# Hyperbolic attention scores on one NeuronCore: the heads' curvature multiplied on GpSimd between two logarithms, in a pipeline with one more stage

## What is computed

```python
def _hyp_attn(q, k, v, curv):
    eps = 1e-06
    tq = jnp.sqrt(1.0 / curv + jnp.sum(q * q, axis=-1, keepdims=True))
    tk = jnp.sqrt(1.0 / curv + jnp.sum(k * k, axis=-1, keepdims=True))
    inner = jnp.einsum('bhtd,bhsd->bhts', q, k) - tq * jnp.swapaxes(tk, -1, -2)
    arg = jnp.maximum(-curv * inner, 1.0 + 1e-07)
    dis = jnp.sqrt(1.0 / curv) * jnp.arccosh(arg)
    scores = 1.0 / (eps + dis) + _causal_bias(...)
    return jnp.einsum('bhts,bhsd->bhtd', jax.nn.softmax(scores, axis=-1), v)
```

## Time and profile before

| | |
|---|---|
| median of 3 runs | 2722.36 us (2722.34 to 2725.09) |
| the profiled execution, its own time | 2718.13 us |
| its span | 2715.2 us |
| busy share PE, DVE, ACT, POOL | 80%, 55%, 52%, 25% |
| granted TensorE clock, mean | 0.839 of full speed |

### The profile page before, as it was taken

The page is one execution under the profiler, slowest core; times in us unless marked ns, Lnnn a source line. Parts: engine busy times, 40 slices in busy tenths (PEclk is TensorE's granted clock), DMA queues, the critical chain, the costliest instruction groups (busy, mean ns, idle before and its releaser), DMA issues. The chain is left out here.

```text
span 2715.2 us, 30081 instructions
## 1 busy us (share of the span) xinstructions
PE 2184.6 (80%) x10649; PEld 840.3 (31%) x10649; DVE 1506.0 (55%) x3298; ACT 1399.8 (52%) x2019; POOL 687.9 (25%) x717
## 2 busy tenths in 40 slices
PE   3799867668999885777898988767799998676689
PEld 1223332124433242222443234212344233321244
DVE  2564456666555255675655625557565543566642
ACT  1245437894234534798324454579632455378932
POOL 1012212332411212233331121133233122123324
PEclk9699876678999986667899988567799998766889
DMA  4200230102500023000431002310051001301012
GB/s 132 65 19 2 69 85 18 34 1 60 137 21 19 1 79 94 25 9 1 114 95 27 1 17 77 79 34 0 5 146 59 19 2 55 93 25 34 1 44 89
DMA packets 67846, 128.32 MB, mean 47 GB/s; under 512 B 11396, under 2 KB 24836, under 8 KB 63076
## 3 DMA queue, kind: packets, MB, share of 16 engines
q1 hardware_dynamic: 67696, 126.40, 16.9%
HBM read 109.99 MB, written 15.20 MB: 46 GB/s over the span
## 5 line engine op out<-in xcount | busy, mean ns | idle before, releaser
L1322 DVE TENSOR_REDUCE mx<-ps 128x1 f32<-128x512 f32 (+3 forms) x1248 | 639.6, 552 | 445.1 <-PE ps L664 346.6
L1070 ACT ACTIVATE pr<-ps 128x1024 f32<-128x1024 f32 (+3 forms) x672 | 515.7, 804 | 435.6 <-PE ps L734 433.4
L661 PE MATMUL ps<-kop,qop 72*128 72x512 bf16 (+6 forms) x1248 | 441.6, 376 | 141.2 <-DVE mx L1322 110.9
L734 PE MATMUL ps<-qop,kop 75*128 75x512 bf16 (+7 forms) x1344 | 408.3, 369 | 113.9 <-DVE wb L1382 40.9
L1609 POOL TENSOR_SCALAR_AFFINE_SELECT pr<-pr 128x512 f32<-128x512 f32 x224 | 146.6, 655 | 833.8 <-ACT pr L1070 833.4
L780 PE MATMUL ps<-pr,vt 128*32 128x512 f32 (+3 forms) x2688 | 344.4, 590 | 6.9 <-POOL pr L1609 6.1
L1129 ACT ACTIVATE pr<-ps 128x512 f32<-128x512 f32 x224 | 133.8, 597 | 343.8 <-PE ps L887 280.2
L661 PEld LDWEIGHTS ps<-kop,qop 72*128 72x128 bf16 (+1 forms) x1248 | 124.2, 102 | 525.1 <-DVE mx L1322 334.2
L734 PEld LDWEIGHTS ps<-qop,kop 75*128 75x128 bf16 (+1 forms) x1344 | 122.2, 105 | 353.0 <-ACT pr L1070 132.1
L897 PE MATMUL ps<-pr,w_down 128*128 128x512 f32 x384 | 197.8, 600 | 3.1 <-POOL pr L1600 3.1
L664 PE MATMUL ps<-maskqk,identb 128*128 128x128 bf16 x832 | 199.0, 247 | 0.0
(11 more groups left out here) (309 smaller groups left out, 2976.3 us busy)
## 6 DMA issues: line engine op xcount, KB each, us to landing
wb<-gates_scratch SPq DMA_DIRECT2D x192, 256.0 KB, 3.4
kop<-kparts_scratch SPq DMA_DIRECT2D x32, 576.0 KB
qop<-qparts_scratch SPq DMA_DIRECT2D x96, 192.0 KB
on<-hmax_scratch SPq DMA_DIRECT2D x8, 1024.0 KB, 5.7
kparts_scratch<-on SPq DMA_DIRECT2D x12, 256.0 KB, 2.9
qparts_scratch<-on SPq DMA_DIRECT2D x12, 256.0 KB, 4.4
qparts_scratch<-wb SPq DMA_DIRECT2D x12, 192.0 KB
kparts_scratch<-wb SPq DMA_DIRECT2D x12, 192.0 KB
```

The costliest lines, as they stand in the source:

```text
L661: mm = pe.matmul(o, qop[0:k, slot(l, u), j, qb * P:(qb + 1) * P], kop[0:k, slot(l, u), j, k0:k0 + wd], start=True, stop=not diag)
L734: mm = pe.matmul(o, kop[0:k, slot(l, u), 2 * pair + j, kb * P:(kb + 1) * P], qop[0:k, slot(l, u), 2 * pair + j, q0:q0 + wd], start=True, s ...
L1070: nc.scalar.activation(pr[:, g % 3, 2 * pair:2 * pair + 2, o0:o0 + wd], ps[:, bank:bank + 2, o0:o0 + wd], ACT.Exp).then_inc(a.exps, 1)
L1322: ins_ = nc.vector.tensor_reduce(mx[:, nth(l, u) % 2, j, qb, col % 2:col % 2 + 1], ps[:, bank, 0:wd], AX.X, ALU.max, negate=True)
```

## The change

`hyp_score` is split. In `hyp_log` ACT takes the first logarithm over both heads; POOL multiplies each head by its factor and adds eps (two `tensor_scalar` of up to 128x512, one semaphore step each, `h_lin`); in the new `hyp_score` ACT takes the second logarithm over both heads without scale or bias, then the exponential. `hyp_log` stays at p+2, the rest goes one position later: `hyp_score` and `hyp_shift` to p+3, `hyp_exp`, `hyp_cut` and `hyp_values` to p+4. On POOL the new pair stands behind the cuts and ahead of the add. The ring keeps five buffers. The outputs of the hyperbolic unit move from positions 12 and 28 to 13 and 29. The number of positions stays at 37, since three ordinary units set it. In the setup, ahead of all batches, two semaphores are folded into others.

```diff
-POSITIONS = (UNITS * NS, max(3 * NS, HYP_POS[-1] + 4) + 1)
+POSITIONS = (UNITS * NS, max(3 * NS, HYP_POS[-1] + 5) + 1)
...
-        outs += [(HYP_POS[2 * (4 + 8 * c) - 1] + 4, HYP_UNIT, c) for c in range(NC)]
+        outs += [(HYP_POS[2 * (4 + 8 * c) - 1] + 5, HYP_UNIT, c) for c in range(NC)]
...
-                    if l and hyp_at(p - 3) != NOBODY:
-                        hyp_values(hyp_at(p - 3))
+                    if l and hyp_at(p - 4) != NOBODY:
+                        hyp_values(hyp_at(p - 4))
...
+                def hyp_log(k):
+                    z = hyp_z(b, k)
+                    act.wait_ge(h_sum, k + 1)
+                    nc.scalar.activation(z, z, ACT.Ln, bias=consts[:, 1:2]).then_inc(h_log, 1)
+
                 def hyp_score(k):
                     z = hyp_z(b, k)
-                    act.wait_ge(h_sum, k + 1)
-                    link(nc.scalar.activation(z, z, ACT.Ln, bias=consts[:, 1:2]))
-                    for i in range(2):
-                        j = 2 * (k % 2) + i
-                        ins_ = nc.scalar.activation(z[:, i], z[:, i], ACT.Ln, scale=hyp[:, 4 + j:5 + j],
-                                                    bias=consts[:, 2:3])
-                    link(ins_)
+                    act.wait_ge(h_lin, 2 * (k + 1))
+                    link(nc.scalar.activation(z, z, ACT.Ln))
                     nc.scalar.activation(z, z, ACT.Exp, scale=-1.0).then_inc(h_score, 1)
...
                     if l:
+                        if hyp_at(p - 4) != NOBODY:
+                            hyp_exp(hyp_at(p - 4))
                         if hyp_at(p - 3) != NOBODY:
-                            hyp_exp(hyp_at(p - 3))
+                            hyp_score(hyp_at(p - 3))
                         if hyp_at(p - 2) != NOBODY:
-                            hyp_score(hyp_at(p - 2))
+                            hyp_log(hyp_at(p - 2))
                         if hyp_at(p - 1) != NOBODY:
                             hyp_root(hyp_at(p - 1))
...
-                    shift = hyp_at(p - 2) if l else NOBODY
+                    shift = hyp_at(p - 3) if l else NOBODY
...
-                if hyp_at(p - 3) != NOBODY:
-                    hyp_cut(hyp_at(p - 3))
+                if hyp_at(p - 4) != NOBODY:
+                    hyp_cut(hyp_at(p - 4))
+                k = hyp_at(p - 2)
+                if k != NOBODY:
+                    pool.wait_ge(h_log, k + 1)
+                    for i in range(2):
+                        j = 2 * (k % 2) + i
+                        z = hyp_z(b, k)[:, i]
+                        nc.gpsimd.tensor_scalar(z, z, hyp[:, 4 + j:5 + j], HYP_EPS, ALU.mult, ALU.add).then_inc(h_lin, 1)
                 k = hyp_at(p - 1)
```

More of the change, by code:

```diff
@@ L399, in adaln_kernel @@
         s_silu = ctx.enter_context(nc.semaphore("s_silu"))
-        s_turn = ctx.enter_context(nc.semaphore("s_turn"))
         s_mm = ctx.enter_context(nc.semaphore("s_mm"))
@@ L404, in adaln_kernel @@
         s_sdve = ctx.enter_context(nc.semaphore("s_sdve"))
-        s_hyp = ctx.enter_context(nc.semaphore("s_hyp"))
         with nc.Block() as block:
@@ L414, in _ @@
                     if l:
-                        sp.wait_ge(s_mm, 1)
+                        sp.wait_ge(s_mm, 2)
                     sp.dma_start(wmod, ins[name]).then_inc(s_wmod, 16)
@@ L434, in _ @@
                 act.wait_ge(s_sdve, 1)
-                nc.scalar.activation(hyp[:, 4:8], hyp[:, 0:4], ACT.Sqrt).then_inc(s_hyp, 1)
+                nc.scalar.activation(hyp[:, 4:8], hyp[:, 0:4], ACT.Sqrt)
             @block.tensor
@@ L440, in _ @@
                 pe.wait_ge(s_load, 16 * len(setup_loads))
-                pe.transpose(ps[:, 7, 0:P], w["maskt"][:], w["ident"][:]).then_inc(s_turn, 1)
+                pe.transpose(ps[:, 7, 0:P], w["maskt"][:], w["ident"][:]).then_inc(s_mm, 1)
                 for l in range(2):
@@ L462, in _ @@
                 nc.vector.reciprocal(hyp[:, 0:4], curvb[:]).then_inc(s_sdve, 1)
-                dve.wait_ge(s_turn, 1)
+                dve.wait_ge(s_mm, 1)
                 nc.vector.tensor_copy(maskqk[:], ps[:, 7, 0:P])
                 for l in range(2):
-                    dve.wait_ge(s_mm, l + 1)
+                    dve.wait_ge(s_mm, l + 2)
                     m = mod[:, l].rearrange("p j b -> p (j b)")
@@ L527, in adaln_kernel @@
         hm_stored, hm_in = sem("hm_stored"), [sem(f"hm_in{c}") for c in range(NC)]
-        h_prod, h_arg, h_sq, h_root, h_sum, h_score, h_sub, h_exp, h_cut, h_pv = (
-            sem("h_" + n) for n in ("prod", "arg", "sq", "root", "sum", "score", "sub", "exp", "cut", "pv"))
+        h_prod, h_arg, h_sq, h_root, h_sum, h_log, h_lin, h_score, h_sub, h_exp, h_cut, h_pv = (
+            sem("h_" + n) for n in ("prod", "arg", "sq", "root", "sum", "log", "lin", "score", "sub", "exp", "cut",
+                                    "pv"))
         y_turn, y_T = sem("y_turn"), sem("y_T")
```

## The result

The changed kernel takes **2677.31 us** (median, 2674.45 to 2683.12, 4 runs) against 2722.35 us before (2711.75 to 2725.09, 4 runs, the same chip): a ratio of **0.9848, 95% interval 0.9825 to 0.987**. Its profiled execution took 2683.12 us, span 2681.4. A second measurement on another chip gave 2672.72 us and a ratio of 0.9823 (0.9798 to 0.9849). So the change is worth 1.5 to 1.8%. A kinder clock isn't the reason: on the second chip the runs of the kernel before with a mean granted clock of 0.838 or more took 2703.21 to 2717.18 us, those of the changed kernel, at 0.838 to 0.842, 2671.02 to 2675.87. Forecast were 2685.0 us, in a range from 2656 to 2714.

What follows compares the result with a forecast made beforehand. ACT was taken to set the pace in thirteen positions a batch, DVE or PE elsewhere. Per batch 7.8 + 1.6 + 1.0 - 1.0 = 9.4 us, 37.6 in all, gave 2685 us, range 2656 to 2714.

Steps and rivals of the forecast that it cites:

- What ACT saves: ACT's score in each half-step: 0.60 us less at any width, a ceiling of 57.6 us over the kernel.
- What of it reaches the end: Second layer's attention, positions 0 to 27: 7.8 us a batch gained where ACT sets the pace, nothing counted elsewhere.
- Thirteen positions: Positions 4 to 6, 12, 13, 16 to 23: ACT sets the pace, each gains 0.60 us.
- The extra stage: Later score gives POOL's add 2.04 us more room: 1.6 us a batch at position 11, plus 1.0 from shifted work.
- filling and draining: Work moved from positions 3 and 4 to 25 to 28: 1.0 us a batch gained, between 0 and 3.
- What POOL adds: POOL's new pair beside ACT's root: 1.3 to 1.5 us taken, bounds 1.3 to 3.5, no time lost.
- What it costs DVE: DVE's two-input instructions held by POOL's use of SBUF: 1.0 us a batch charged.
- Only the later half counts: PE's values follow closely in positions 4 to 6, 12, 13; only 16 to 23 gain, 19 us, 2703; chance 0.18.
- DVE takes over: POOL holds DVE's L1395 or L1387 in each position, making the kernel slower, 2729 or 2765 us; chance 0.12.
- The whole saving: DVE and PE follow ACT everywhere, so all 57.6 us and position 11's wait come through, 2658 us; chance 0.15.
- no change: Products and reductions catch up everywhere and extra POOL work eats the rest, 2719 to 2726 us; chance 0.10.
- The sum: Gain per batch over all terms: 7.8 + 1.6 + 1.0 - 1.0 = 9.4 us, 37.6 in all; chance 0.45.

Runs made afterwards that it cites:

- experiment 2: The kernel before the change, with ACT's second logarithm taken once over both heads, factor and eps left out: 2704.66 us, ratio 0.9941.
- experiment 3: The changed kernel with POOL's pair over only 8 columns of each head: 2672.81 us, ratio 0.9835 to the kernel before.
- experiment 5: The changed kernel with the hyperbolic unit's own maxima for the next batch taken one position later: 2662.65 us, ratio 0.9805 to the kernel before.

## Why the prediction was right in its number, and where not in its steps

- **What ACT saves: right.** 0.60 us a half-step at the full width; 7.88 us a position, where nothing else comes last. The busy time fell by 54.5 of 57.6 us.
- **What of it reaches the end: wrong in the second half.** "Thirteen positions" was the step that failed. For 4 to 6, 12 and 13 it held with a surplus. For 16 to 23 I had 4.8 us a batch, and got -1.3 and 0.1. I read "no wait" on ACT as "ACT sets the pace". At position 22 DVE's argument had been ready for only 0.03 to 0.31 us, so of all that ACT saves in 16 to 22 little could reach the end unless DVE came earlier with it (1.1 us in experiment 2, nothing in the change). And in the second batch the round through PE and DVE was 8.96 and 9.23 us long, longer than ACT's 8.48, hidden by a distance that ran down from 1.56 us to 0.03. The means of DVE and POOL in the earlier trace rows couldn't show either: they end at position 19, and come from the first batch, where the clock was mostly high (0.83, 1.00 and 0.87 from root to root). A wait of zero says that an engine comes last, not by how much.
- **The extra stage: right in direction, too small, and position 11 for another reason.** Position 11 gave 2.03 for 1.6, but not by its wait: ACT waits 1.38 us there after (0.86 for POOL, 0.52 for DVE) and 1.61 before. What left the position is work, since a narrow score stands there in place of the wide one. Position 3 gave 2.0 where I took 1.0 for all filling and draining; positions 12 and 13 gave another 0.9 over their 0.60 each. With four half-steps in flight, more of those in flight at the start of a wide block are narrow ones or none, and the wide ones end in positions 14, 15, 24 and 25, which gained too. The run with the stage alone says the same: 4.7 us a batch for 2.6. So filling and draining was the term that was too small. The count has a slip: "these 11 half-steps" are ten by the positions named, and position 3 is the eleventh.
- **What POOL adds: right.** 0.69 us a piece uncontended, for 0.65 to 0.75 forecast, but 0.87 to 1.14 on the mean. So the pair takes 1.7 to 2.3 us, over my value, inside my bounds. No one waits for it. The Trainium skill, "GPSIMD Engine Reference", section 3.1, has 769 ns for 512 elements with one input; the trace has 690 ns in the clear, somewhat less.
- **What it costs DVE: wrong about who pays.** I charged DVE 1.0 us a batch. The pair's own pieces were stretched, to 1.77 us at most, and DVE's busy time didn't move against before. The first collision, at position 14, stands as in the earlier trace rows: DVE's L1396 took 2.51 us at 505.76 beside POOL's add. Only the doubled pair made DVE pay.
- **The rivals.** "Only the later half counts" named one agent rightly, PE at a low granted clock, in the wrong half. "DVE takes over" would have needed 1.31 us of hold in each position, and the pair's work can't be told from none (experiment 3). Of its signs one came all the same: ACT does wait for L1388 in positions 16 to 20, though L1388 and L1396 are no longer than before. "The whole saving" fails in 16 to 23, and "no change" by 45 us.
- **The sum.** 9.4 us a batch forecast, 7.1 and 10.2 in the two traces, 11.3 by the medians. The excess of the stage (2.6 forecast, 4.7 measured alone) stood in for the missing later half. That the number came out is in good part luck, and the two single runs say so: 16 us for the saving of 0.47 us, where thirteen positions make 24, and 19 us for the stage, where I had 10.

## What to carry to other kernels

Where one engine runs without a wait, read how long each of its inputs had been ready when it took them, in every batch and in the stretches with the lowest clock, down to the next place where another engine comes last. The smallest of these distances is what a faster engine can be sure to gain up to there, and more comes only if the other engine gets earlier with it; a saving in each of seven positions is not seven savings. When a step of a chain is handed to another engine, consider moving its consumer a stage later with it: here the hand-over then cost no engine any time, while in the one order tried without the stage ACT's and DVE's queues closed a round that made the kernel 2.7% slower. Work added to an engine with room may be free once and dear the second time, when it pushes the next instruction into another engine's way.

## What the runs showed of the hardware

- The same program at the same positions took 7.88 us or 9.0 to 9.3, as the granted clock in them and ahead of them went, and the four stretches differ by 12.4 us in two executions. Ahead of the long periods of the second batch, in position 15, PE was busy for 9.10 of 9.85 us, all at the lower level (0.50). Within one kernel the runs with a higher mean granted clock are mostly the shorter ones: experiment 5 ran from 2652.89 us at 0.846 to 2682.94 us at 0.825.
- At the lower level eight and four matmuls of values took 1.94 and 1.92 us, at the upper 1.06 and 1.03.
- A POOL `tensor_scalar` with a factor from memory takes 0.69 us for 128x512 and 0.37 for 128x128 in the clear. In the kernel 36 of 96 pieces of 128x512 took over 0.75 us, up to 1.77, while DVE's L1388 and L1396 took over 1.5 us in 6 of 192 cases, as before the change.
